# A graph kernel on one Trainium2 core: the first block issues three head weights and the indices only, the other loads follow in the main block, and ten node steps stand between gathering and messages

## The chip, the cores and the metric

One core of one Trainium2 chip. The metric is the device time of one launch in microseconds (us), lower is better. The engines: PE (TensorE, matrix products), DVE (VectorE), ACT (ScalarE), POOL (GpSimd) and SP (SyncE, which here only issues DMAs). Each has its own queue of instructions, in program order; they meet through semaphores.

## What is computed

Two layers of a graph network on 50,000 nodes with 256 features each and 12,500 edges, sorted by destination. The reference, cut:

```python
# layer 0: attention of 4 heads over the edges
h = einsum('ni,hid->nhd', x, W)
e = leaky(einsum('ehd,hd->eh', h[src], a_src) + einsum('ehd,hd->eh', h[dst], a_dst))
alpha = exp(minimum(e - segment_max(e)[dst], 20)); alpha /= segment_sum(alpha)[dst] + 1e-8
x = layernorm(x + segment_sum(alpha * h[src]).reshape(N, 256) @ W_out)
# layer 1: messages with edge attributes, a gate and a skip
m = x @ W_n2m.T; q, k, v = (m @ Wi.T + bi for i in 'qkv'); e = (edge_attr @ W_edge.T) @ We.T
out = segment_sum((v[src] + e) * segment_softmax(q[dst] . (k[src] + e) / sqrt(32)))
x_r = m @ Wskip.T + bskip
beta = sigmoid(concat(out, x_r, out - x_r) @ Wbeta.T)
x = layernorm(x + (beta * x_r + (1 - beta) * out) @ W_m2n.T)
```

Most nodes are the destination of no edge. For them both layers reduce to a layernorm, a product with 256 x 257 fixed weights, a sigmoid gate and a second layernorm.

## The kernel before

**Two kinds of work.** The *edge work* goes over 100 tiles of 125 edges, in stages: `Score` (gather rows of x by source and by destination with two indirect DMAs of POOL per tile, L824; transpose on PE, L847; project, L857 and L859; ACT copies to ST, L870, and to the store, L879; SP writes the gathered rows back, L835), a first `Softmax` (soft1), `Gather` (sum the weighted rows per destination, add to x, SP stores the rows, L1186), `Message` (gather again by source, L1308; normalize, L1473; keys, values, queries, L1368 to L1391), a second `Softmax` (soft2) and `Output`. The *node work* (`Nodes`) treats all 50,000 nodes as if they had no edge, in 196 steps of 256 rows: SP loads (L635), DVE measures (L763, L778), POOL takes the roots (L666, L671), ACT or DVE normalizes (L683 and L715, or L784), PE transposes (L734) and multiplies (L744), ACT and DVE gate and add (L696, L770), SP stores nine steps later (L651). Nodes with edges are overwritten by `Output` at the end. Step s loads the rows of step s + 2 into one of 12 slots; that load waits until the store that last used the slot has landed, and that store was issued in the step before.

**Set-up.** `head_pass` is the first block (L161 to L250). SP issues 24 loads: indices, the head weights `wh` and `attn`, all weights of layer 1, W_out, and, after a wait for DVE's memsets (L194), the borders of the tiles; ACT issues five loads of biases. PE turns the index rows and ACT copies them (L208, L209). A block ends for all engines when the last of them is done. All weights count on one semaphore, `c.ldd` (LOADS, L157). In the main block `Weights` (called `made`) derives the fused weights in five steps 0 to 4 between DVE and PE: DVE step 0 (L325 to L336, makes HEADS_READY), PE step 1 (transposes, L288 to L293), DVE step 1 (L338 to L353), PE step 2 (L300 to L302), DVE step 2 (L356 to L361), PE step 3 (L306, L307), DVE step 3 (L365), PE step 4 (L311 to L315), DVE step 4 (L370 to L388, makes NODES_READY, then ALL_READY). The first node product on PE waits for NODES_READY. `Masks` and `Positions` make the borders' masks and row positions on DVE; `Finder` looks up source rows. They use a scratch area in the store that the tiles from 72 on (FREE) overwrite.

**The order.** One plan, a list of (part, step), is made ahead by `order_of`, and every engine emits its instructions in this order. In the first stage `start_of` puts the steps of made, masks and positions at score steps written out by hand (MADE_AT, MASKS_AT, POSITIONS_AT, L1722 to L1724) and blends the first 74 node steps in from score step NODES_FROM on, the finder from FINDER_FROM on. For each later stage `blend` spreads a number of node steps (NODE_SHARE: 74 in the first stage, then 10, 66, 45, 10) evenly among the stage's own steps. The message stage has steps -6 to 102; at step -5 (A = 5) POOL waits until all rows of the gather stage are stored (L1302) and gathers the tiles' tails (L1305), and SP waits for these, writes them (L1335), waits for that write and then loads tile 0 (L1338). SP meets its node loads and stores in the same queue, in plan order.

```python
plan = start_of(entries[score], entries[finder], entries[nodes][0:at], entries[made], entries[masks], entries[positions])
for count, group in zip(share[1:], ((soft1,), (gather,), (message,), (soft2,))):
    lists = [entries[nodes][at:at + count]] + [entries[n] for n in group]
```

Of the kernel before, what the change touches and what calls it, by code (L numbers as in the profile page):

```python
# [153 lines left out]
        self.picked = take(TILES, P)  # L154


LOADS = 16 * (1 + 4 + 6 + 3 + 1 + 3 + 5)  # L157
EDGE_LOADS = 16 * 4


def head_pass(nc, c, ctx, io):  # L161
# [9 lines left out]
    with nc.Block() as block:  # L171
        @block.sync
        def _(sp):
            with nc.allow_non_contiguous_dma(reason="400 first and last dst of the tiles and a few short weight rows, once"):
                sp.dma_start(w.dsti, rows).then_inc(idx_loads, 16)
                sp.dma_start(w.srci, src.rearrange("(t e) -> t e", e=EDGES)).then_inc(idx_loads, 16)
                for k in range(2):
                    sp.dma_start(c.wh[:, k, 0:D].rearrange("p (h d) -> p h d", h=H),
                                 io["L0_gnn_W"][:, k * P:(k + 1) * P, :].rearrange("h i d -> i h d")).then_inc(c.ldd, 16)
                sp.dma_start(w.attn.rearrange("p h d -> p (h d)"),  # L180
                             io["L0_gnn_attn"].rearrange("(a h) d -> a (h d)", a=1).to_broadcast([P, H * 2 * HD])).then_inc(c.ldd, 16)
                for k, name in enumerate(("Wq", "Wk", "Wv", "Wskip")):
                    sp.dma_start(w.w_sq[:, k, :], io["L1_gnn_" + name]).then_inc(c.ldd, 16)
                for k in range(2):
                    sp.dma_start(w.w_m2n[:, k, :], io["L1_gnn_W_m2n"][k * P:(k + 1) * P, :]).then_inc(c.ldd, 16)
                sp.dma_start(w.w_e, io["L1_gnn_We"]).then_inc(c.ldd, 16)
                for k in range(3):
                    sp.dma_start(w.beta[:, k:k + 1], io["L1_gnn_Wbeta"][:, k * DM:(k + 1) * DM].rearrange("a d -> d a")).then_inc(c.ldd, 16)
                sp.dma_start(w.w_n2m, io["L1_gnn_W_n2m"]).then_inc(c.ldd, 16)
                for k in range(2):  # L190
                    sp.dma_start(w.w_edge[:, k, :], io["L1_gnn_W_edge"]).then_inc(c.ldd, 16)
                for k in range(2):
                    sp.dma_start(c.wo[:, k, :], io["L0_gnn_W_out"][k * P:(k + 1) * P, :]).then_inc(c.ldd, 16)
                sp.wait_ge(dve_done, 4)  # L194
                sp.dma_start(w.previ[1:TILES, :], rows[0:TILES - 1, EDGES - 1:EDGES]).then_inc(c.edge_loads, 16)
                sp.dma_start(w.nexti[0:TILES - 1, :], rows[1:TILES, 0:1]).then_inc(c.edge_loads, 16)
                for k, e in ((0, 0), (1, EDGES - 1)):
                    sp.dma_start(w.edgei[:, k, :], dst.rearrange("(a t e) -> a t e", a=1, e=EDGES)[:, :, e].to_broadcast([H, TILES])).then_inc(c.edge_loads, 16)

        @block.scalar  # L200
        def _(act):
            with nc.allow_non_contiguous_dma(reason="one bias column"):
                for out, name in ((w.bq_xr[:, 0:DM], "bq"), (w.bq_xr[:, DM:2 * DM], "bskip"), (w.b_kv[:, 0:DM], "bk"), (w.b_kv[:, DM:2 * DM], "bv")):
                    act.dma_start(out, io["L1_gnn_" + name].rearrange("(a d) -> a d", a=1).to_broadcast([P, DM])).then_inc(c.ldd, 16)
                act.dma_start(w.bs_cols[:, 0:1], io["L1_gnn_bskip"].rearrange("(d a) -> d a", a=1)).then_inc(c.ldd, 16)
            act.wait_ge(turned, 1)
            for k, out in enumerate((c.src_col, c.dst_col)):
                act.activation(out[:, :], c.psum[:, 0, k * 256:k * 256 + TILES], ACT.Copy).then_inc(turned, 1)  # L208
            act.activation(c.src_next[:, :], c.psum[:, 0, 0:TILES], ACT.Copy, bias=1.0).then_inc(turned, 1)  # L209
            act.wait_ge(turned, 4)  # L210

        @block.gpsimd
        def _(pool):
            own = Own(pool, pool_done)
            own(pool.memset(c.ident[:, :], 0.0))
            own.done()
            own(pool.affine_select(out=c.ident[:, :], in_=c.ident[:, :], compare_op=ALU.not_equal, fill=1.0,
                                   base=0, pattern=[[-1, P]], channel_multiplier=1))
            own(pool.memset(w.zero, 0.0))
            own(pool.memset(w.mean_w, 1.0 / D))  # L220
            own(pool.memset(c.half[:, :], -0.5))
            own(pool.memset(c.half5[:, :], -0.5))
            own(pool.memset(c.we2[:, :, :], 0.0))
            own(pool.iota(w.posi, [[1, EDGES]], base=1, channel_multiplier=P))
            own(pool.iota(w.basei, [[1, 1]], base=0, channel_multiplier=P))
            own(pool.iota(w.placei, [[1, EDGES]], base=1, channel_multiplier=0))
            own(pool.iota(c.own_pos[:, :], [[P, TILES]], base=0, channel_multiplier=1))
            own.done()

        @block.vector  # L230
# [12 lines left out]

        @block.tensor
        def _(pe):
            pe.wait_ge(pool_done, 2)
            pe.wait_ge(dve_done, 7)
            for k in range(2):
                last = pe.transpose(c.psum[:, 0, k * 256:k * 256 + TILES], w.row[:, k, :], c.ident[0:TILES, 0:TILES])
            last.then_inc(turned, 1)  # L250


class Weights:
# [2 lines left out]
    HEADS_READY, NODES_READY, ALL_READY = 1, 2, 3  # L256
    SPREAD, FUSED, MIXED = 20, 25, 28

    def __init__(self, nc, c, ctx):
        self.c = c  # L260

        def sem(name):
            return c.semaphore(nc, ctx, "weights_" + name)

        self.pe_done, self.own_sem, self.ready = (sem(n) for n in ("pe_done", "own_sem", "ready"))

    def sync(self, sp):
        def emit(s):
            return
        return emit  # L270

    def pool(self, pool):
# [10 lines left out]
    def tensor(self, pe):  # L283
        c, ps, w = self.c, self.c.psum, self.c.scratch

        def emit(s):
            if s == 1:
                pe.wait_ge(c.ldd, LOADS)  # L288
                for k in range(4):
                    pe.transpose(ps[:, 0, k * P:(k + 1) * P], w.w_sq[:, k, :], c.ident[:, :])  # L290
                for k in range(2):
# [27 lines left out]
    def vector(self, dve):  # L319
# [3 lines left out]

        def emit(s):
            if s == 0:  # L325
                dve.wait_ge(c.ldd, LOADS)
                for half, out in ((0, c.wh[:, :, D:HP]), (1, c.w_ad[:, :, :])):
                    own.done()
                    for k in range(2):
# [5 lines left out]
                own.done()  # L335
                dve.sem_inc(self.ready, 1)  # L336
            if s == 1:
                own(dve.tensor_tensor(w.wb, w.beta[:, 1:2], w.beta[:, 2:3], ALU.subtract))  # L338
                own(dve.tensor_tensor(w.wa, w.beta[:, 0:1], w.beta[:, 2:3], ALU.add))
                dve.wait_ge(self.pe_done, 1)  # L340
# [51 lines left out]
class Masks:  # L392
# [41 lines left out]

    def vector(self, dve):
        c, w = self.c, self.c.scratch
        own = Own(dve, self.own_sem)

        def emit(s):
            if s == 0:  # L440
# [45 lines left out]
class Positions:  # L486
# [3 lines left out]
    def __init__(self, nc, c, ctx, masks):  # L490
# [2 lines left out]
        def sem(name):  # L493
            return c.semaphore(nc, ctx, "positions_" + name)

        self.own_sem, self.asks, self.answers, self.ready, self.table = (sem(n) for n in ("own_sem", "asks", "answers", "ready", "table"))

    def sync(self, sp):
        def emit(s):
# [30 lines left out]

    def vector(self, dve):
        c, ps, w = self.c, self.c.psum, self.c.scratch
        own = Own(dve, self.own_sem)

        def emit(s):
            if s == 0:
# [711 lines left out]
class Message:  # L1248

    A = 5  # L1250
    B = 4
    FIRST, LAST = -6, TILES + 3

    def __init__(self, nc, c, ctx, io, made, positions, gather, finder):
        self.c, self.made, self.positions, self.gather, self.finder = c, made, positions, gather, finder
# [386 lines left out]
def main_pass(nc, c, io, out):  # L1642

    with ExitStack() as ctx:
# [4 lines left out]

        c.load_keeps = load_keeps  # L1650

        made = Weights(nc, c, ctx)
        masks = Masks(nc, c, ctx)
        positions = Positions(nc, c, ctx, masks)
        nodes = Nodes(nc, c, ctx, io["x"], out, made, NODE_NORMED, NODE_SCALED)
# [43 lines left out]
                    emits[n](s)  # L1699


NODE_SHARE = (74, 10, 66, 45, 10)
NODE_NORMED = ["A" if 74 <= s < 84 or s >= 186 else "AD"[s % 2] if s >= 84 else "D" for s in range(NSTEPS)]
NODE_SCALED = ["AD"[s % 2] if s < 66 else "A" for s in range(NSTEPS)]

# [1 line left out]
def order_of(parts, share):  # L1707
# [3 lines left out]
    entries = [[(n, s) for s in range(p.FIRST, p.LAST)] for n, p in enumerate(parts)]  # L1711
    at = share[0]
    plan = start_of(entries[score], entries[finder], entries[nodes][0:at], entries[made], entries[masks], entries[positions])
    for count, group in zip(share[1:], ((soft1,), (gather,), (message,), (soft2,))):
        lists = [entries[nodes][at:at + count]] + [entries[n] for n in group]
        at += count
        plan += [entry for _, entry in blend(lists)]
    assert at == len(entries[nodes])
    return plan + entries[output]


MADE_AT = (-5, -5, 0, 2, 4)  # L1722
MASKS_AT = (1, 6, 8, 10, 12)
POSITIONS_AT = (14, 16, 18, 20)  # L1724
NODES_FROM, FINDER_FROM = 2, 22


def start_of(score, finder, nodes, made, masks, positions):
# [22 lines left out]
def build(nc, io, out):  # L1751
    with ExitStack() as ctx:
        c = Core()
        c.ldd = c.semaphore(nc, ctx, "ldd")
        c.edge_loads = c.semaphore(nc, ctx, "edge_loads")

        def sb(name, shape, dt=F32):
# [85 lines left out]
```

## Time and profile before

| | us |
|---|---|
| median of 3 runs | 1377.34 (1364.89 to 1383.67) |
| the profiled execution | 1366.76, its span 1365.0 |
| PE busy in the span | 1197.2 |
| DVE, ACT, POOL busy | 1039.6, 810.9, 842.9 |

The profile shows one execution. Its span runs from the first to the last instruction; all times of the timeline count from its start. "Busy" leaves out waiting and issuing. Stages, roughly: start and scores to 400 us, soft1 to 450, gather to 733, messages to 1117, soft2 to 1150, output to the end. A row of the timeline merges several instructions of one line (xN).

### The profile page before, as it was taken

To read this page: it belongs to the slowest core of one execution; us is meant where nothing else is said; L and a number is where in the kernel's file an instruction comes from. 1 tells how busy PE (TensorE), PEld (TensorE's weight loads), DVE (VectorE), ACT (ScalarE), POOL (GpSimd) and SP (SyncE) were. 2 spreads that over 40 slices of the span, in tenths; PEclk is the share of its full clock that TensorE was granted. 3 is DMA by queue.
4 is the path that set the end of the run, shared out by engine and by line. 5 is a ranking of instruction groups with operands and counts; after the bars stand their busy time and mean duration, and the time that the engine had idled before them with its cause. 6 is when DMAs were issued, how large, how long until landed. Compare 5 with 4: busy or idle time off the path is not lost. (4 is left out here: it accounts for less than half of the span.)

```text
span 1365.0 us, 29010 instructions
## 1 busy us (share of the span) xinstructions
PE 1197.2 (88%) x7386; PEld 1061.5 (78%) x7386; DVE 1039.6 (76%) x3852; ACT 810.9 (59%) x2583; POOL 842.9 (62%) x1060
## 2 busy tenths in 40 slices
PE   3799999999995889899896999999999992988881
PEld 2688998989984777777775899999999982877771
DVE  3476777777779788898885888888888876877771
ACT  0366666666667756566565666666666675555652
POOL 4688888888843544455543666666666632377775
PEclk9899999999999999999999999999999996999996
DMA  6668888888853678787786766666666622555541
GB/s 161 193 186 262 285 253 274 264 272 264 268 185 116 185 228 238 236 246 240 240 243 202 222 209 198 192 201 197 199 197 185 200 93 98 158 176 169 172 155 58
DMA packets 208940, 277.09 MB, mean 203 GB/s; under 512 B 40060, under 2 KB 140563, under 8 KB 208777
## 3 DMA queue, kind: packets, MB, share of 16 engines
q1 hardware_dynamic: 188793, 224.13, 52.9%
q0 software_dynamic: 19264, 50.85, 13.1%
q8 instruction: 63, 1.03, 0.3%
q14 instruction: 100, 0.82, 0.2%
q10 hardware_dynamic: 720, 0.26, 0.1%
HBM read 159.73 MB, written 117.12 MB: 203 GB/s over the span
## 5 line engine op out<-in xcount | busy, mean ns | idle before, releaser
L744 PE MATMUL banks<-m_ext,node_XT 128*128 128x257 f32 x1568 | 377.9, 384 | 0.0
L744 PEld LDWEIGHTS banks<-m_ext,node_XT 128*128 128x128 f32 x1568 | 286.3, 193 | 32.9
L770 DVE SCALAR_TENSOR_TENSOR node_X<-banks,node_be,node_X 128x256 f32<-128x256 f32 x392 | 169.7, 474 | 79.2 <-ACT node_be L696 53.8
L671 POOL TENSOR_TENSOR node_r<-node_vv,half 128x4 f32<-128x4 f32 (+1 forms) x202 | 215.3, 1066 | 17.1 <-ACT node_X L683 0.3
L702 ACT ACTIVATE node_XT<-banks 128x512 f32<-128x512 f32 x196 | 117.2, 598 | 139.4 <-PE banks L734 125.2
L666 POOL TENSOR_SCALAR node_vv<-node_mv 128x4 f32<-128x4 f32 (+1 forms) x202 | 57.0, 282 | 212.4 <-DVE node_mv L778 196.9
L763 DVE BATCH_NORM_STATS2 node_st<-node_X 128x6 f32<-128x256 f32 x392 | 145.7, 413 | 20.7 <-DMA node_X<-in_x 19.3
L709 ACT ACTIVATE node_sq<-node_X 128x256 f32<-128x256 f32 x392 | 158.0, 409 | 0.0
L734 PE MATMUL banks<-ident,node_X 128*128 128x128 f32 x784 | 122.2, 279 | 28.5 <-DVE node_X L784 14.1
L683 ACT ACTIVATE node_X<-node_X,node_r 128x256 f32<-128x256 f32 x326 | 146.0, 496 | 1.4 <-POOL node_r L671 1.4
L824 POOL DMA_INDIRECT ring<-in_x,src_col x100 | 106.9, 1069 | 35.2 <-issue 14.2
L734 PEld LDWEIGHTS banks<-ident,node_X 128*128 128x128 f32 x784 | 95.8, 149 | 41.5 <-issue 19.5
L1531 POOL DMA_INDIRECT out<-ring,last_col x100 | 102.5, 1025 | 35.3 <-issue 21.9
L1308 POOL DMA_INDIRECT ring<-rows,src_pos x100 | 105.7, 1057 | 22.3 <-issue 20.4
L824 POOL DMA_INDIRECT ring<-in_x,dst_col x100 | 97.3, 973 | 31.4 <-issue 31.4
L857 PE MATMUL banks<-wh,ST 128*128 128x260 f32 x400 | 107.5, 392 | 9.1 <-ACT store L879 8.0
L870 ACT ACTIVATE ST<-banks 128x512 f32<-128x512 f32 x100 | 59.7, 597 | 86.9 <-PE banks L847 38.6
L1383 PE MATMUL banks<-w_kv,ST 128*128 128x256 f32 x400 | 103.1, 380 | 0.2 <-DVE store L1436 0.2
L1217 PE MATMUL banks<-wo,AT 128*128 128x256 f32 x400 | 102.9, 380 | 0.0
L1243 DVE TENSOR_TENSOR_SCAN AT<-MB,AT,banks 128x128 f32<-128x128 f32 x198 | 83.9, 465 | 19.1 <-PE banks L1210 15.2
L784 DVE TENSOR_SCALAR node_X<-node_X,node_mv,node_r 128x256 f32<-128x256 f32 x250 | 90.5, 403 | 0.0
L1568 PE MATMUL banks<-w_out,S 128*128 128x256 f32 x200 | 63.4, 399 | 24.3 <-DVE AT L1621 19.4
(262 smaller groups left out, 2773.4 us busy)
## 6 DMA issues: line engine op xcount, KB each, us to landing
node_X<-in_x SPq DMA_DIRECT2D x196, 256.0 KB
out<-node_X SPq DMA_DIRECT2D x196, 256.0 KB
ring<-rows SPq DMA_DIRECT2D x300, 128.0 KB
rows<-ring SPq DMA_DIRECT2D x100, 256.0 KB
rows<-ring SPq DMA_DIRECT2D x200, 128.0 KB
MB<-keeps SPq DMA_DIRECT2D x40, 320.0 KB, 5.5
MB<-picks SPq DMA_DIRECT2D x50, 128.0 KB
MB<-in_src SPq DMA_DIRECT2D x25, 195.3 KB
```

Source lines behind the costliest of these rows:

```text
L671: pool.tensor_tensor(r[:, s % 4, NT * lo:NT * hi], v, self.c.half[:, NT * lo:NT * hi], ALU.pow).then_inc(self.roots, 1)
L683: last = eng.activation(row, row, ACT.Identity, scale=rz)
L702: act.activation(self.XT[:, n % 2, :], c.psum[:, 4, 0:NT * D], ACT.Copy, bias=1.0).then_inc(self.xt_ready, 1)
L709: last = act.activation(self.sq[:, k, :], X[:, n % U, k, :], ACT.Square, scale=1.0 / D ** 0.5, accum_out=self.mv[:, s % 4, 1, k, 1:2])
L734: last = pe.transpose(ps[:, 4, k * D + h * P:k * D + (h + 1) * P], self.X[:, n % U, k, h * P:(h + 1) * P], c.ident[:, :])
L744: last = pe.matmul(ps[:, NT * o + k, 0:D + 1], self.XT[:, o, k * D + h * P:k * D + (h + 1) * P], c.m_ext[:, h, :], start=(h == 0), stop=(h ...
L763: last = dve.bn_stats(st[:, s % 2, k, :], X[:, s % U, k, :])
L770: last = dve.scalar_tensor_tensor(out=X[:, n % U, k, :], in0=ps[:, b + k, 0:D], scalar=self.be[:, n % 4, k:k + 1], in1=X[:, n % U, k, :], ...
L824: pool.indirect_dma_start(out=c.ring[:, n % R, side, :], out_offset=None, in_=self.x, in_offset=bass.IndirectOffsetOnAxis(ap=col[:, n:n + ...
L857: pe.matmul(ps[:, 6, 0:HP], c.ST[:, o, h * P:(h + 1) * P], c.wh[:, h, :], start=(h == 0), stop=(h == 1))
L1308: pool.indirect_dma_start(out=c.ring[:, n % R, 1, :], out_offset=None, in_=c.rows, in_offset=bass.IndirectOffsetOnAxis(ap=c.src_pos[:, n:n ...
L1383: pe.matmul(ps[:, 6, 0:2 * DM], c.ST[:, o, h * P:(h + 1) * P], c.w_kv[:, h, :], start=(h == 0), stop=(h == 1))
```

## The change

The first block keeps, on SP, the indices, `wh` and `attn` (counted on a new semaphore, `head_loads`), and ACT issues what PE's step 1 of the weights reads (`turn_loads`; the two parts of W_m2n in one DMA). The other 16 loads (12 on `ldd`, four of borders on `edge_loads`) are issued by SP in the main block, as step 0 of made, which stands ahead of score step -5. PE's step 1 waits for `turn_loads`, DVE's step 0 for `head_loads`, DVE's step 1 for `ldd`. The hand-written places move. The node steps of the message stage, 45, are split: 4 alone behind the gather stage, 6 blended with message steps -6 to -1, 35 with the rest. Masks and positions share one counting semaphore.

```diff
-LOADS = 16 * (1 + 4 + 6 + 3 + 1 + 3 + 5)
+HEAD_LOADS = 16 * 3
+TURN_LOADS = 16 * 7
+LOADS = 16 * 12
@@ head_pass, SP
                 for k in range(2):
                     sp.dma_start(c.wh[:, k, 0:D]...,
-                                 ...).then_inc(c.ldd, 16)
+                                 ...).then_inc(c.head_loads, 16)
                 sp.dma_start(w.attn..., ...
-                             ...).then_inc(c.ldd, 16)
-                ...
-                sp.wait_ge(dve_done, 4)
-                ...
+                             ...).then_inc(c.head_loads, 16)
@@ head_pass, ACT
-                for out, name in ((w.bq_xr[:, 0:DM], "bq"), (w.bq_xr[:, DM:2 * DM], "bskip"), (w.b_kv[:, 0:DM], "bk"), (w.b_kv[:, DM:2 * DM], "bv")):
-                    act.dma_start(out, ...).then_inc(c.ldd, 16)
-                act.dma_start(w.bs_cols[:, 0:1], ...).then_inc(c.ldd, 16)
+            for k, name in enumerate(("Wq", "Wk", "Wv", "Wskip")):
+                act.dma_start(w.w_sq[:, k, :], io["L1_gnn_" + name]).then_inc(c.turn_loads, 16)
+            act.dma_start(w.w_m2n, io["L1_gnn_W_m2n"].rearrange("(k p) d -> p k d", p=P)).then_inc(c.turn_loads, 16)
+            act.dma_start(w.w_e, io["L1_gnn_We"]).then_inc(c.turn_loads, 16)
+            act.dma_start(w.w_n2m, io["L1_gnn_W_n2m"]).then_inc(c.turn_loads, 16)
@@ Weights.sync
+            if s == 0:
+                    for k in range(3):
+                        sp.dma_start(w.beta[:, k:k + 1], ...).then_inc(c.ldd, 16)
+                    sp.dma_start(w.bs_cols[:, 0:1], ...).then_inc(c.ldd, 16)
+                    for k in range(2):
+                        sp.dma_start(w.w_edge[:, k, :], ...).then_inc(c.ldd, 16)
+                    sp.dma_start(w.previ[1:TILES, :], ...).then_inc(c.edge_loads, 16)
+                    sp.dma_start(w.nexti[0:TILES - 1, :], ...).then_inc(c.edge_loads, 16)
+                    for k, e in ((0, 0), (1, EDGES - 1)):
+                        sp.dma_start(w.edgei[:, k, :], ...).then_inc(c.edge_loads, 16)
+                    for out, name in (... "bq", "bskip", "bk", "bv" ...):
+                        sp.dma_start(out, ...).then_inc(c.ldd, 16)
+                    for k in range(2):
+                        sp.dma_start(c.wo[:, k, :], ...).then_inc(c.ldd, 16)
@@ Weights.tensor, s == 1
-                pe.wait_ge(c.ldd, LOADS)
+                pe.wait_ge(c.turn_loads, TURN_LOADS)
@@ Weights.vector
             if s == 0:
-                dve.wait_ge(c.ldd, LOADS)
+                dve.wait_ge(c.head_loads, HEAD_LOADS)
             if s == 1:
+                dve.wait_ge(c.ldd, LOADS)
@@ Positions
-        own = Own(dve, self.own_sem)
+        own = self.masks.own
@@ Message
-    FIRST, LAST = -6, TILES + 3
+    FIRST, EARLY, LAST = -6, 0, TILES + 3
@@ order_of
-NODE_SHARE = (74, 10, 66, 45, 10)
+NODE_SHARE = (74, 10, 66, 4, 6, 35, 10)
-    for count, group in zip(share[1:], ((soft1,), (gather,), (message,), (soft2,))):
-        lists = [entries[nodes][at:at + count]] + [entries[n] for n in group]
+    first = Message.EARLY - Message.FIRST
+    stages = ((entries[soft1],), (entries[gather],), (), (entries[message][:first],), (entries[message][first:],), (entries[soft2],))
+    for count, group in zip(share[1:], stages):
+        lists = [entries[nodes][at:at + count]] + [e for e in group]
@@ the places in the first stage
-MADE_AT = (-5, -5, 0, 2, 4)
-MASKS_AT = (1, 6, 8, 10, 12)
-POSITIONS_AT = (14, 16, 18, 20)
-NODES_FROM, FINDER_FROM = 2, 22
+MADE_AT = (-5, -3, 0, 1, 3)
+MASKS_AT = (4, 7, 9, 11, 14)
+POSITIONS_AT = (13, 15, 17, 20)
+NODES_FROM, FINDER_FROM = 3, 20
```

## Rows read from the trace of the kernel before

**Rows 1.** The page, first part: busy time, share of the span, instructions.

```profile
PE 1197.2 (88%) x7386; PEld 1061.5 (78%) x7386; DVE 1039.6 (76%) x3852; ACT 810.9 (59%) x2583; POOL 842.9 (62%) x1060
```

**Rows 2.** Windows: stretch, its length, busy us (count) of PE, PEld, DVE, ACT, POOL, clock, DMA, GB/s.

```profile
30.00:40.00 10.00, 3.32 (x19) 2.48 (x17) 1.48 (x7) 0.60 (x1) 6.65 (x7) 0.91 0.95 312
...
740.00:750.00 10.00, 0.46 (x3) 0.20 (x2) 2.42 (x10) 0.98 (x4) 4.42 (x6) 0.74 0.69 195
...
900.00:1000.00 100.00, 100.00 (x706) 93.82 (x705) 87.44 (x366) 63.13 (x192) 63.74 (x80) 1.00 0.67 198
```

**Rows 3.** Timeline from 0 us: start, duration, engine, line, tiles, [idle before <-releaser].

```profile
3.11 1.28 ACT L208 ACT_TABLE_LOAD   x1 [3.11 <-issue]
...
5.55 1.29 SPq L183 DMA_DIRECT2D store<-in_L_gnn_Wskip  x1
...
13.70 0.97 SPq L198 DMA_DIRECT2D store<-in_dst  x2
...
15.20 0.76 DVE L330 TENSOR_TENSOR store<-wh,store 128x256 f32<-128x256 f32 x2 [10.39 <-PEq L171]
...
15.98 1.16 POOL L824 DMA_INDIRECT ring<-in_x,src_col  x1 [13.26 <-POOLq L171]
```

**Rows 4.** DMA issues by tile: engine, count, size, median us to landing.

```profile
wo<-in_L_gnn_W_out SPq DMA_DIRECT2D x2, 128.0 KB, 2.2
```

**Rows 5.** Timeline, 18 to 60 us: weights, gathers, stores, first node step.

```profile
18.46 0.16 DVE L338 TENSOR_TENSOR store<-store 128x1 f32<-128x1 f32 x1
...
31.14 1.11 PE L306 MATMUL banks<-w_out,store 128*128 128x257 f32 x4
...
37.53 0.95 POOL L824 DMA_INDIRECT ring<-in_x,dst_col  x1 [0.30 <-issue]
...
41.39 0.39 ACT L879 ACTIVATE store<-banks 128x260 f32<-128x260 f32 x1 [7.85 <-remote]
...
42.82 6.59 SPq L835 DMA_DIRECT2D rows<-ring  x2
...
57.32 0.63 PE L734 MATMUL banks<-ident,node_X 128*128 128x128 f32 x4 [0.61 <-DVE node_X L784]
```

**Rows 6.** Timeline of SP's queue, 732 to 746 us.

```profile
732.80 0.33 SPq L635 DMA_DIRECT2D node_X<-in_x  x1
...
736.31 0.33 SPq L635 DMA_DIRECT2D node_X<-in_x  x1
736.74 0.38 SPq L651 DMA_DIRECT2D out<-node_X  x1
...
739.92 0.35 SPq L635 DMA_DIRECT2D node_X<-in_x  x1
...
741.97 0.30 SPq L1335 DMA_DIRECT2D rows<-AT  x1
745.30 0.32 SPq L1338 DMA_DIRECT2D ring<-rows  x1
```

**Rows 7.** Timeline of POOL, 733 to 738 us.

```profile
737.71 1.15 POOL L1305 DMA_INDIRECT AT<-rows,tail_pos  x1 [2.36 <-issue]
```

**Rows 8.** Timeline of DVE and PE, 735 to 763 us.

```profile
735.69 0.75 DVE L763 BATCH_NORM_STATS2 node_st<-node_X 128x6 f32<-128x256 f32 x2 [0.67 <-DMA node_X<-in_x]
...
747.54 0.75 DVE L1446 BATCH_NORM_STATS2 message_st<-ring 128x6 f32<-128x256 f32 x2 [10.17 <-DMA ring<-rows]
...
755.12 0.38 PE L1368 MATMUL banks<-ident,ring 128*128 128x128 f32 x2
...
760.13 0.60 PE L734 MATMUL banks<-ident,node_X 128*128 128x128 f32 x4
...
762.31 0.38 PE L1368 MATMUL banks<-ident,ring 128*128 128x128 f32 x2
```

**Rows 9.** Timeline of PE, 417 to 422 us (the softmax stage).

```profile
417.76 0.63 PE L734 MATMUL banks<-ident,node_X 128*128 128x128 f32 x4 [0.58 <-issue]
...
420.89 0.63 PE L734 MATMUL banks<-ident,node_X 128*128 128x128 f32 x4 [0.76 <-issue]
```

More of the change, by code:

```diff
@@ L173, in _ @@
         def _(sp):
-            with nc.allow_non_contiguous_dma(reason="400 first and last dst of the tiles and a few short weight rows, once"):
+            with nc.allow_non_contiguous_dma(reason="short rows of the head weights"):
                 sp.dma_start(w.dsti, rows).then_inc(idx_loads, 16)
@@ L178, in _ @@
                     sp.dma_start(c.wh[:, k, 0:D].rearrange("p (h d) -> p h d", h=H),
-                                 io["L0_gnn_W"][:, k * P:(k + 1) * P, :].rearrange("h i d -> i h d")).then_inc(c.ldd, 16)
+                                 io["L0_gnn_W"][:, k * P:(k + 1) * P, :].rearrange("h i d -> i h d")).then_inc(c.head_loads, 16)
                 sp.dma_start(w.attn.rearrange("p h d -> p (h d)"),
-                             io["L0_gnn_attn"].rearrange("(a h) d -> a (h d)", a=1).to_broadcast([P, H * 2 * HD])).then_inc(c.ldd, 16)
@@ L182, in _ @@
[L182 to L193, printed above, removed]
-                sp.wait_ge(dve_done, 4)
-                sp.dma_start(w.previ[1:TILES, :], rows[0:TILES - 1, EDGES - 1:EDGES]).then_inc(c.edge_loads, 16)
@@ L196, in _ @@
-                sp.dma_start(w.nexti[0:TILES - 1, :], rows[1:TILES, 0:1]).then_inc(c.edge_loads, 16)
-                for k, e in ((0, 0), (1, EDGES - 1)):
-                    sp.dma_start(w.edgei[:, k, :], dst.rearrange("(a t e) -> a t e", a=1, e=EDGES)[:, :, e].to_broadcast([H, TILES])).then_inc(c.edge_loads, 16)
+                             io["L0_gnn_attn"].rearrange("(a h) d -> a (h d)", a=1).to_broadcast([P, H * 2 * HD])).then_inc(c.head_loads, 16)
         @block.scalar
         def _(act):
-            with nc.allow_non_contiguous_dma(reason="one bias column"):
-                for out, name in ((w.bq_xr[:, 0:DM], "bq"), (w.bq_xr[:, DM:2 * DM], "bskip"), (w.b_kv[:, 0:DM], "bk"), (w.b_kv[:, DM:2 * DM], "bv")):
-                    act.dma_start(out, io["L1_gnn_" + name].rearrange("(a d) -> a d", a=1).to_broadcast([P, DM])).then_inc(c.ldd, 16)
-                act.dma_start(w.bs_cols[:, 0:1], io["L1_gnn_bskip"].rearrange("(d a) -> d a", a=1)).then_inc(c.ldd, 16)
+            for k, name in enumerate(("Wq", "Wk", "Wv", "Wskip")):
+                act.dma_start(w.w_sq[:, k, :], io["L1_gnn_" + name]).then_inc(c.turn_loads, 16)
@@ L257, with __init__ @@
     SPREAD, FUSED, MIXED = 20, 25, 28
-    def __init__(self, nc, c, ctx):
-        self.c = c
+    def __init__(self, nc, c, ctx, io):
+        self.nc, self.c, self.io = nc, c, io
         def sem(name):
@@ L267, in sync @@
     def sync(self, sp):
+        nc, c, w, io = self.nc, self.c, self.c.scratch, self.io
+        dst = io["dst"]
+        rows = dst.rearrange("(t e) -> t e", e=EDGES)
         def emit(s):
-            return
+            if s == 0:
+                with nc.allow_non_contiguous_dma(reason="400 first and last dst of the tiles and a few short weight rows, once"):
+                    for k in range(3):
+                        sp.dma_start(w.beta[:, k:k + 1], io["L1_gnn_Wbeta"][:, k * DM:(k + 1) * DM].rearrange("a d -> d a")).then_inc(c.ldd, 16)
+                    sp.dma_start(w.bs_cols[:, 0:1], io["L1_gnn_bskip"].rearrange("(d a) -> d a", a=1)).then_inc(c.ldd, 16)
+                    for k in range(2):
+                        sp.dma_start(w.w_edge[:, k, :], io["L1_gnn_W_edge"]).then_inc(c.ldd, 16)
+                    sp.dma_start(w.previ[1:TILES, :], rows[0:TILES - 1, EDGES - 1:EDGES]).then_inc(c.edge_loads, 16)
+                    sp.dma_start(w.nexti[0:TILES - 1, :], rows[1:TILES, 0:1]).then_inc(c.edge_loads, 16)
+                    for k, e in ((0, 0), (1, EDGES - 1)):
+                        sp.dma_start(w.edgei[:, k, :], dst.rearrange("(a t e) -> a t e", a=1, e=EDGES)[:, :, e].to_broadcast([H, TILES])).then_inc(c.edge_loads, 16)
+                    for out, name in ((w.bq_xr[:, 0:DM], "bq"), (w.bq_xr[:, DM:2 * DM], "bskip"), (w.b_kv[:, 0:DM], "bk"), (w.b_kv[:, DM:2 * DM], "bv")):
+                        sp.dma_start(out, io["L1_gnn_" + name].rearrange("(a d) -> a d", a=1).to_broadcast([P, DM])).then_inc(c.ldd, 16)
+                    for k in range(2):
+                        sp.dma_start(c.wo[:, k, :], io["L0_gnn_W_out"][k * P:(k + 1) * P, :]).then_inc(c.ldd, 16)
         return emit
@@ L436, in vector @@
         c, w = self.c, self.c.scratch
-        own = Own(dve, self.own_sem)
+        own = self.own = Own(dve, self.own_sem)
         def emit(s):
@@ L494, in sem @@
             return c.semaphore(nc, ctx, "positions_" + name)
-        self.own_sem, self.asks, self.answers, self.ready, self.table = (sem(n) for n in ("own_sem", "asks", "answers", "ready", "table"))
+        self.asks, self.answers, self.ready, self.table = (sem(n) for n in ("asks", "answers", "ready", "table"))
     def sync(self, sp):
@@ L532, in vector @@
         c, ps, w = self.c, self.c.psum, self.c.scratch
-        own = Own(dve, self.own_sem)
+        own = self.masks.own
         def emit(s):
@@ L1650, in main_pass @@
         c.load_keeps = load_keeps
-        made = Weights(nc, c, ctx)
+        made = Weights(nc, c, ctx, io)
         masks = Masks(nc, c, ctx)
@@ L1753, in build @@
         c = Core()
-        c.ldd = c.semaphore(nc, ctx, "ldd")
+        c.ldd, c.head_loads, c.turn_loads = (c.semaphore(nc, ctx, n) for n in ("ldd", "head_loads", "turn_loads"))
         c.edge_loads = c.semaphore(nc, ctx, "edge_loads")
```

## The prediction

> **What bounds the kernel now.** Read first the busy shares, then the windows, then the two places in time that the diff touches. TensorE (PE) is busy 1197.2 of 1365.0 us, 88% [rows 1]; in the message stage a window of 100 us shows it at 100.00 us [rows 2]. So in the long stages PE is the bound, and PE work can't be made shorter by moving it, only moved into holes. The windows show two holes that the diff touches. One is the start: PE works 3.32 us between 30 and 40 us, while the DMA engines are 0.95 busy [rows 2]. The other is the change from gathering to messages: PE works 0.46 us between 740 and 750 [rows 2].
>
> Of the start the timeline gives the parts. The first block ends when SP has issued its last load (13.70 + 0.97 = 14.67), and DVE starts the next block at 15.20, POOL its first gather at 15.98 [rows 3]. Then a chain runs through the weights: DVE L338 at 18.46, PE L306 at 31.14 [rows 5]. ACT's L879 waits for PE's L859, which the trace puts before L306; yet ACT is released only at 41.39, with 7.85 us of idle time that the profile puts down to no instruction ("remote") [rows 5]. I read this as PE's results coming out late, or not being seen; the trace doesn't say why. It ends 2.9 us after POOL's last gather of the first burst (37.53 + 0.95 = 38.48) [rows 5]. Steady work begins with the first node step, at 57.32 [rows 5].
>
> Of the second hole: after the gather stage SP stands in a chain of DMAs. The tails are gathered (POOL, 737.71) [rows 7], SP stores them 4.26 us later (741.97), waits for the store and loads tile 0 at 745.30 [rows 6], DVE has it at 747.54 after 10.17 us of idle time, and PE's first message is at 755.12 [rows 8].
>
> **The start, step by step.** SP's block now ends after five issues instead of 24. ACT issues seven loads, where it had five. One issue takes from 0.49 (0.97 for two, L198) to 1.29 us (L183 at 5.55) [rows 3], so seven end between 4.1 and 9.7 us. Behind them stand the table load, 1.28 us [rows 3], and three short activations; with about 2.3 us for these the block ends between 6.4 and 12. I take 6.8, near the short issue, since ACT's queue has fewer packets ahead of it than SP's had. With the same 0.53 us from block end to DVE (14.67 to 15.20) and 0.78 more to POOL [rows 3], gathers begin at 8.1, 7.9 us earlier (bounds 2.7 and 8.3).
>
> What doesn't come earlier is the chain of weights. Its second step (DVE L338) now waits for the twelve loads on ldd, and these stand among 16 issues at the head of SP's queue in the main block: 7.3 + 16 x 0.49 = 15.1, and the last (wo) needs 2.2 us to land [rows 4], 17.3 in all. Before, the step began at 18.46 [rows 5]. The 16 issues now run beside the gathers, and where the DMA engines are full SP took 6.59 us for two issues (L835 at 42.82) [rows 5]. I take 18.5 for the step, no change; bounds 17.3 and, at 1.1 us an issue, 27. All that SP has behind these issues (stores of gathered tiles, node loads) is due only when gathers have landed, near 15 us, so the 16 cost it nothing if they end there. The head weights (HEADS_READY) come earlier, but PE's first product stands behind the second weight step, so nobody uses that.
>
> The gain is the burst. POOL runs 18 gathers from 15.98 to 38.48, 1.25 us each; with NODES_FROM at 3 it runs 20 before its first node step, from 8.1 to 33.1. If the late results end 2.9 us after it, as they do now, ACT goes on at 36.0 instead of 41.39: 5.4 us earlier. Behind that the last weight step stands one score step earlier, and one more tile stands ahead of the first node step; I set these equal. So the first node step comes at 51.9 instead of 57.32, and PE is full from there: minus 5.4. Bounds: if the results aren't late at all, 8.7 us go (32.7, the end of L306 and L307, to 41.4) and somewhat more with the earlier last step, minus 11; if the late loads take 27, plus 6 (8.5 later, less an estimated 2.5, since the burst is over by then and its late results no longer add).
>
> **The change of stages, step by step.** Before, three node steps stand ahead of message step 0 and 42 behind it; now ten and 35. In the full message stage a node step costs PE 2.18 us (L734 at 760.13 to the next tile's L1368 at 762.31) [rows 8]; seven fewer save 15.3 us there. That is the gain side, and it is firm, since PE is at 100% (bounds 14 and 16.5).
>
> Against it: ten node steps with nothing else run at their own pace p. SP sets it: the load of a step waits for the store of the step before to land, and 736.74 to 739.92 is 3.18 us; step to step it is 3.5 to 3.6 (732.80, 736.31, 739.92) [rows 6]. In the softmax stage, without the gather stage's rows, steps follow at 3.13 us (417.76 to 420.89) [rows 9]. I take p = 3.3, bounds 2.9 and 3.9.
>
> Follow SP. Its last step of the gather stage is at 736.31; step 155, behind which the tails now stand, ends at 737.1 + 6p = 756.9 (six steps on). POOL gathers the tails after its part of step 155, near 752, and they land by then too. Then, as before, 3.33 us for the store of the tails (741.97 to 745.30), 0.8 us to the next node load, one p for the load after it, 2.89 us until DVE has that (732.80 to 735.69) [rows 6, 8], and about 4 us for DVE's rest of node and message steps up to PE's step 0 (half of the 7.58 from 747.54 to 755.12). Sum: 737.1 + 3.3 + 0.8 + 2.9 + 4.1 + 7p = 748.2 + 7p = 771.3. Before it was 755.12: 16.2 us later, against 15.3 saved: plus 0.9. With p = 2.9 it is minus 1.8, with 3.9 plus 5. So ten steps fill the hole, but node steps alone run at 3.3 us where PE would do them in 2.18 between messages, and that eats what the hole gives.
>
> The Trainium skill has a rule here: by "DMA: Bandwidth & Descriptors", section "Anatomy of one DMA", a DMA takes about 2.0 us plus its bytes at 436 GB/s (fitted there on DMAs that POOL issues), which for 256 KB would be 2.6 us instead of the row's 3.18, p near 3.0 and the stage minus 1; the trace is slower than the rule in this place.
>
> **At nothing.** The masks, positions and finder move by a few score steps; all stand beside a PE that is full, and are first needed at tile 72, hundreds of us later (price if that failed: a few us, once). The shared count of positions and masks, two semaphores more and one less, and the joined m2n load cost nothing that I can see; bounds plus and minus 0.5.
>
> **Sum.** Minus 5.4 plus 0.9 is minus 4.5: of the profiled execution's 1366.8 us, 1362.3. That execution is 10.6 us below the median of the runs shown; on the median, 1377.3, it is 1372.8.
>
> **Rivals.** (a) PE's late results go away with the new order of work, since made step 3 no longer stands behind tile 1: minus 11 and plus 0.9, 1367. For it: the later parts of the trace show no such wait. Against: the same burst of gathers and stores runs over the same chain, only earlier. (b) The second hole fills well: with the lighter traffic stores land sooner, p is near 2.8, PE's step 0 at 767.8: minus 2.6 there and minus 5.4 at the start, 1369. For it: 3.13 in the softmax stage; against: messages' loads go through the same queue. (c) The late loads are slowed by the gathers. It decides from the landing of wo: beyond 18.5 us each us is lost, beyond about 24 (the issues at 0.95 us each) the start is slower than before. At 1.1 us each the start is plus 6, with plus 0.9 the time is 1384, slower than before. For it: the 0.95 DMA share and SP's 6.59 us; against: 16 loads are few bytes. (d) The start does nothing: the late results end at 41.4 whatever comes before: 1378.
>
> **How the numbers follow.** Forecast 0.42, (a) 0.15, (b) 0.15, (c) 0.13, (d) 0.15. All lie within 1% of each other, and the runs shown of the kernel before spread over 1364.9 to 1383.7. The range is 1359 to 1385: (a) at its low end with some spread, (c) at its high end. About 2% (27.5 us) is what a measurement of this kernel can tell from no change; none of the cases reaches it. Faster by more than that, 0.05, if (a) and (b) hold together and more; slower, 0.04; within, 0.91.
>
> **What would show it.** Right: POOL's first gather near 8 us; DVE L338 near 18.5 though DVE's first step starts near 10; the long wait of ACT L879 ending near 36; the first node step near 52; SP's node loads about 3.3 us apart through the second hole, PE's first message step about 35 us after the gather stage's last node load, and the message stage some 15 us shorter from its step 0. Wrong: a first node step beyond 57, or before 49; node steps apart by more than 3.9 or less than 2.9; PE idle for 5 us in one piece in the second hole; a message stage in which PE has idle time, so that seven fewer node steps save less than 14.

## The result and the profile after

The changed kernel takes 1378.66 us in the median of 12 runs (1372.98 to 1382.6), against 1373.88 for the kernel before, measured beside it in 12 runs (1364.89 to 1383.82). The ratio is 1.0071, with an interval of 1.0053 to 1.009: slower by 0.7%, within the 2% that I had given 0.91, and inside the range of 1359 to 1385, but on the other side of no change than the forecast (1372.8 of 1377.3, a ratio of 0.997). The runs of the kernel before lie in two groups, and 1.0071 is the changed kernel's mean, 1378.3, over that of the seven runs up to 1377.34, 1368.6, while the medians of all runs give 1.0035. So the size of the loss isn't firm from these runs alone; that there is one rests also on the experiments below.

The profiled execution took 1382.16 us, with a span of 1380.3; that of before was 1366.76, near the low end of its runs. The two traces differ by 15 us, the medians by 4.8, so the traces serve for the order of things and the durations of steps, not for the sum.

The page of the changed kernel, busy time; PE has 12.7 us more than in [rows 1], for the same instructions:

```profile
PE 1209.9 (88%) x7386; PEld 1066.7 (77%) x7386; DVE 1044.2 (76%) x3852; ACT 809.5 (59%) x2583; POOL 842.5 (61%) x1060
```

Its windows, in the columns of [rows 2]:

```profile
30.00:40.00 10.00, 2.16 (x7) 1.64 (x6) 2.10 (x5) 0.60 (x1) 1.89 (x2) 0.61 0.93 339
...
740.00:750.00 10.00, 6.55 (x35) 5.10 (x34) 5.72 (x24) 7.00 (x24) 3.96 (x6) 1.00 0.52 159
...
900.00:1000.00 100.00, 99.90 (x706) 93.43 (x705) 86.39 (x363) 61.06 (x183) 63.74 (x78) 1.00 0.66 194
```

The first hole is emptier than before (PE 2.16 of 10 us instead of 3.32). The second is filled, though not full: 6.55 instead of 0.46. The message stage is as full as it was, with the same 706 matmuls in 100 us.

**The start.** Timeline of the changed kernel, 0 to 60 us, against [rows 3, 5]:

```profile
6.38 1.29 SPq L262 DMA_DIRECT2D store<-in_L_gnn_Wbeta  x3
...
7.20 1.31 POOL L829 DMA_INDIRECT ring<-in_x,src_col  x1 [4.47 <-POOLq L173]
...
14.38 0.91 SPq L273 DMA_DIRECT2D wo<-in_L_gnn_W_out  x2
15.34 6.35 SPq L840 DMA_DIRECT2D rows<-ring  x3
...
21.62 0.16 DVE L343 TENSOR_TENSOR store<-store 128x1 f32<-128x1 f32 x1 [11.45 <-DMA wo<-in_L_gnn_W_out]
...
31.45 0.95 POOL L829 DMA_INDIRECT ring<-in_x,dst_col  x1 [0.30 <-issue]
...
35.80 0.42 DVE L362 COPY store<-banks 128x256 f32<-128x256 f32 x1 [11.14 <-remote]
35.86 0.60 ACT L875 ACTIVATE ST<-banks 128x512 f32<-128x512 f32 x1 [29.90 <-remote]
...
37.99 2.08 PE L310 MATMUL banks<-w_out,store 128*128 128x257 f32 x4 [7.84 <-DVE we L366]
...
58.37 0.63 PE L739 MATMUL banks<-ident,node_X 128*128 128x128 f32 x4 [0.49 <-DVE node_X L789]
```

POOL gathers 8.8 us earlier than before (7.20 for 15.98), and SP has issued the last late load at 15.29. But DVE's second weight step, L343 here, waits 11.45 us for `wo` and starts at 21.62, where L338 started at 18.46: 3.2 us later. The late results are there again ("remote"), and end at 35.86. PE's step 3 of the weights, L310, which stood ahead of them at 31.14, now stands behind them at 37.99: it waits for DVE's L366, and DVE saw PE's step 2 only at 35.80 (L362). The first node step comes 1.05 us later than before, not 5.4 earlier.

**The change of stages.** SP's queue in the changed kernel, 736 to 769 us, against [rows 6]:

```profile
736.05 0.33 SPq L640 DMA_DIRECT2D node_X<-in_x  x1
...
743.17 0.33 SPq L640 DMA_DIRECT2D node_X<-in_x  x1
743.61 0.38 SPq L656 DMA_DIRECT2D out<-node_X  x1
746.77 0.33 SPq L640 DMA_DIRECT2D node_X<-in_x  x1
747.20 0.38 SPq L656 DMA_DIRECT2D out<-node_X  x1
750.77 0.33 SPq L640 DMA_DIRECT2D node_X<-in_x  x1
...
758.87 0.35 SPq L640 DMA_DIRECT2D node_X<-in_x  x1
...
759.79 0.31 SPq L1340 DMA_DIRECT2D rows<-AT  x1
762.50 0.32 SPq L1343 DMA_DIRECT2D ring<-rows  x1
...
763.35 0.42 SPq L640 DMA_DIRECT2D node_X<-in_x  x1
...
768.13 0.33 SPq L640 DMA_DIRECT2D node_X<-in_x  x1
```

POOL's gather of the tails, DVE's first look at a message tile and PE's first message there, against [rows 7, 8]:

```profile
752.99 1.15 POOL L1310 DMA_INDIRECT AT<-rows,tail_pos  x1 [0.22 <-issue]
...
764.56 0.75 DVE L1451 BATCH_NORM_STATS2 message_st<-ring 128x6 f32<-128x256 f32 x2 [0.71 <-DMA ring<-rows]
...
775.18 0.44 PE L1373 MATMUL banks<-ident,ring 128*128 128x128 f32 x2 [2.23 <-DVE ring L1478]
```

From 736.05, the last load of the gather stage, to 758.87, the last one ahead of the tails, there are six node steps, 3.8 us each (3.6 to 4.0, and the last 4.5); the next takes 4.8 (763.35 to 768.13). A store stands right behind each load, and each load waits for the store that was issued behind the load before it. The waits of SP's queue from 728 to 785 us, as a sum, a count and the longest:

```profile
SPq L640 <- DMA out<-node_X: 33.9, 13, 3.6
```

PE's message step 0 starts at 775.18 instead of 755.12, 20.1 us later. From there to the end of the last message tile's transposes it is 347.6 us instead of 358.7: 11.1 us are saved.

### The profile page after: what moved, and what is told of

The parts are those of the page before. It is cut to its first block and busy times, and to the rows that moved or that the text cites. A ratio compares the mean times of both kernels' runs of the same rounds, so it can differ in the third digit from the quotient of the medians.

```text
span 1380.3 us, 29009 instructions
## 1 busy us (share of the span) xinstructions
PE 1209.9 (88%) x7386; PEld 1066.7 (77%) x7386; DVE 1044.2 (76%) x3852; ACT 809.5 (59%) x2583; POOL 842.5 (61%) x1060
## 5 line engine op out<-in xcount | busy, mean ns | idle before, releaser
L1573 PE MATMUL banks<-w_out,S 128*128 128x256 f32 x200 | 64.8, 407 | 27.1 <-DVE AT L1626 20.2
```

## The experiments

They ran in three comparisons (`start_only`, `stages_only`, `start_gated` and `before_again`, then the two other edits of the start and the two with `AHEAD = 1`, then the last four), each on a chip of its own. The kernel before took 1343.66, 1341.09 and 1342.1 us there, against 1373.88 above; so I take them for other chips than the one of the two kernels above, which isn't on record. Ratios are against its runs in the same comparison, and marks in time are compared among these runs alone.

**The start and the regrouping, each alone.** `start_only` is the changed kernel with the stages of before:

```diff
-NODE_SHARE = (74, 10, 66, 4, 6, 35, 10)
+NODE_SHARE = (74, 10, 66, 45, 10)
-    stages = (..., (entries[gather],), (), (entries[message][:first],), (entries[message][first:],), ...)
+    stages = (..., (entries[gather],), (entries[message],), ...)
```

> The change with its stage split undone (45 node steps in the message stage again): only the new start. Theory A (the loss is the change of stages): 0 to +4 us against before, ratio 0.998 to 1.003; first message transpose on PE about 26 us after the gather stage's last sum, as before. Theory B (the loss is the start, the late loads): +7 to +11 us, ratio near 1.007.

It took 1348.1 us: 1.0039 [1.0022, 1.0056]. `stages_only` is the kernel before with the same edit the other way round (and `EARLY = 0`).

> The kernel before with only the node steps regrouped (4, 6, 35). Theory A: +7 to +10 us, ratio near 1.006; PE's first message transpose about 45 us after the gather stage's last sum instead of 26, and the message stage from there shorter by 11 to 12 us. Theory B: 0 to +2 us.

It took 1349.25 us: 1.005 [1.0033, 1.0067]. Both halves cost time. Their sum, 0.89%, lies in the interval of the whole change, 0.53% to 0.9%; it is more than the 0.35% of the medians, so this is a rough check only. For reference, `before_again` is the kernel before, unchanged, traced beside them.

> The kernel before, unchanged, for a second trace: its runs fall into two groups, near 1367 and near 1382 us. If this one is of the slow group, the stage in which it loses shows where the 15 us come from; expected: the output stage (195 us in the first trace, 201 in that of the changed kernel), and a start within 2 us of the first trace.

It took 1344.41 us, one run, and the 15 runs of the kernel before beside it lie between 1339.07 and 1346.6; so where the 15 us that I asked for come from stays open. Its start isn't within 2 us of the first trace either, and the trace has no late results at all. PE in `before_again`, the first node step:

```profile
44.29 0.63 PE L734 MATMUL banks<-ident,node_X 128*128 128x128 f32 x4 [0.61 <-DVE node_X L784]
```

That is 13 us earlier than in [rows 5], though its DVE L338 starts at 18.6 as there. So my 5.4 us rested on a disturbance that isn't there in every execution. In `start_only` the chain is undisturbed too, and yet the first node step comes at 52.18, 7.9 us later than in `before_again`: the second weight step starts 3.8 us later (22.44 for 18.62), and from there to the first node step it takes 4.1 us longer. Its DVE, POOL and PE:

```profile
22.44 0.19 DVE L343 TENSOR_TENSOR store<-store 128x1 f32<-128x1 f32 x1 [12.11 <-DMA wo<-in_L_gnn_W_out]
...
47.52 0.34 POOL L671 TENSOR_SCALAR node_vv<-node_mv 128x2 f32<-128x2 f32 x1 [15.34 <-DVE node_mv L783]
...
52.18 0.63 PE L739 MATMUL banks<-ident,node_X 128*128 128x128 f32 x4 [0.46 <-DVE node_X L789]
```

PE's first message, in `before_again` and in `stages_only`:

```profile
746.66 0.43 PE L1368 MATMUL banks<-ident,ring 128*128 128x128 f32 x2
```

```profile
766.76 0.69 PE L1368 MATMUL banks<-ident,ring 128*128 128x128 f32 x2 [3.72 <-DVE ring L1473]
```

The last rows of the gather stage are done at 719.0 in `stages_only` and at 719.1 in `before_again`. From there to message step 0 it is 47.8 us against 27.5: 20.2 longer. From step 0 to the end of the last message transposes it is 344.0 us against 357.9: 14.0 saved. The net of 6.3 fits the 6.7 us of the ratio.

**Are the gathers what delays the loads and the results?** `start_gated` is `start_only` with POOL held after two tiles until PE has done step 3 of the weights.

```diff
+                if n == 2:
+                    pool.wait_ge(self.made.pe_done, 3)
```

> start_only, but POOL holds the gathers of tiles 2 and up until PE's third weight step is done. Theory A1 (PE's results come out late because the burst of gathers, stores and node loads fills the DMA engines): no idle time of ACT or DVE put down to nothing above 1 us in the first 60 us, wo landed by 18 us instead of 21.6, PE's fourth weight step near 36 us instead of 45; in all 3 to 8 us faster than start_only if the gathers held back don't run late. Rival A2 (late results come with PE's cold clock or the profile, not with the burst): the same 5 us of late results near 30 us, and the time no better than start_only.

It took 1353.36 us: 1.0073 [1.0055, 1.0092]. DVE's second weight step came at 19.65 instead of 22.44, so with four gathers beside the loads instead of a full burst `wo` lands 2.8 us sooner, at the same time of issue; but the tiles then come late, the first node step at 54.58. On the late results it says nothing, since `start_only` has none either, and the 3 to 8 us that I expected didn't come.

**What of the start costs?** Two edits of `start_only`. `start_old_places` puts the hand-written places back to those of before:

```diff
-MADE_AT = (-5, -3, 0, 1, 3)
-MASKS_AT = (4, 7, 9, 11, 14)
-POSITIONS_AT = (13, 15, 17, 20)
-NODES_FROM, FINDER_FROM = 3, 20
+MADE_AT = (-5, -5, 0, 2, 4)
+MASKS_AT = (1, 6, 8, 10, 12)
+POSITIONS_AT = (14, 16, 18, 20)
+NODES_FROM, FINDER_FROM = 2, 22
```

> start_only with the hand-written places of before (weights, masks, positions, node and finder start). Theory P (half of the start's loss is the places: one more tile and the masks ahead of the first node steps while POOL's gathers stop at the same wait): first node transpose on PE about 4 us earlier than in start_only (48 instead of 52.2), 2 to 4 us faster than start_only. Theory L (all of it is the late landing of the loads): within 1 us of start_only, DVE's second weight step at 22.4 in both.

It took 1342.22 us: 1.0007 [0.9993, 1.0021], no difference from before. Issue to landing in it, and then its POOL and PE:

```profile
wo<-in_L_gnn_W_out SPq DMA_DIRECT2D x2, 128.0 KB, 6.7
```

```profile
36.41 0.24 POOL L671 TENSOR_SCALAR node_vv<-node_mv 128x2 f32<-128x2 f32 x1 [6.70 <-DVE node_mv L783]
...
46.95 0.63 PE L739 MATMUL banks<-ident,node_X 128*128 128x128 f32 x4 [0.62 <-DVE node_X L789]
```

`wo` took 6.7 us to land, where [rows 4] has 2.2. The second weight step is as late as in `start_only` (22.1), but from there to the first node step it is 24.8 us instead of 29.7. With the new places the last step of the weights stands ahead of the first node step in DVE's queue; POOL stands 15.34 us at that node step's root instead of 6.70, and gathers nothing from 32.19 to 49.00. The run moved all the places at once; that this one makes the difference is read from the traces, not tested alone. `start_split_loads` gives the loads that DVE's step 1 doesn't read (four biases and W_out) a semaphore of their own, waited for at its step 4:

```diff
-LOADS = 16 * 12
+LOADS = 16 * 6
+REST_LOADS = 16 * 6
+            if s == 4:
+                dve.wait_ge(c.rest_loads, REST_LOADS)
```

> start_only, but the biases and W_out count on a semaphore of their own that only DVE's last weight step waits for; its second step waits for the six loads issued first. Theory L: that step comes near 12 to 14 us instead of 22.4, PE's second step near 16 instead of 25.6, and the start ends 8 to 12 us earlier than in start_only, 4 to 8 us ahead of before (ratio 0.994 to 0.997). Theory D (the DMA engines are full from 15 us on and the gathers and node loads set the start): the weight steps come early but the first node transpose stays above 46 and the time within 3 us of start_only.

It took 1338.22 us: 0.9966 [0.9946, 0.9986], faster than before and 0.7% faster than `start_only`. Waits of DVE up to 62 us in `start_only` and in `start_split_loads`:

```profile
DVE store L343 <- DMA wo<-in_L_gnn_W_out: 12.1, 1, 12.1
```

```profile
DVE store L344 <- DMA store<-in_L_gnn_W_edge: 0.6, 1, 0.6
```

One wait of 12.1 us becomes 0.6; the step starts at 10.80, and the first node step follows at 41.03:

```profile
10.80 0.16 DVE L344 TENSOR_TENSOR store<-store 128x1 f32<-128x1 f32 x1 [0.60 <-DMA store<-in_L_gnn_W_edge]
```

```profile
41.03 0.63 PE L741 MATMUL banks<-ident,node_X 128*128 128x128 f32 x4 [0.56 <-DVE node_X L791]
```

**Is it the store ahead of each load that sets the pace?** `AHEAD = 1` makes step s load the rows of step s + 1, so the slot's last store was issued one step earlier than with 2 and has a step more to land. `before_ahead1` is the kernel before with it, `stages_ahead1` is `stages_only` with it.

```diff
-    AHEAD = 2
+    AHEAD = 1
```

> The kernel before with node loads one step ahead, as the reference for stages_ahead1. Theory S: both softmax stages and the tail of gathering a little faster, 2 to 6 us less than before; then stages_ahead1 loses less against this one (0 to +3 us) than stages_only against before (+6.7). Theory E: within 2 us of before.

> stages_only with node loads issued one step ahead instead of two, so that a load's slot was stored two steps before and SP doesn't wait for that store to land. Theory S (the pace of node steps that stand alone, 3.6 us, is SP's: load after the landing of the last store): pace 2.7 to 3.1 us between gathering and messages, PE's first message transpose 4 to 6 us earlier than in stages_only (767), 4 us or more faster than stages_only. Theory E (the engines' own chain DVE, POOL, ACT, PE sets the pace): pace 3.4 to 3.6 as before, same time or a little slower, DVE waiting for loads.

They took 1332.53 us, 0.9927 [0.9902, 0.9951], and 1332.5 us, 0.9932 [0.9911, 0.9953]; on the kernel before that is more than the 2 to 6 us expected. The waits of SP's queue from 400 to 1100 us, in `before_again`, `stages_only`, `before_ahead1` and `stages_ahead1`:

```profile
SPq L635 <- DMA out<-node_X: 124.7, 70, 5.1
```

```profile
SPq L635 <- DMA out<-node_X: 150.2, 78, 5.0
```

```profile
SPq L635 <- DMA out<-node_X: 2.7, 2, 2.0
```

```profile
SPq L635 <- DMA out<-node_X: 3.9, 3, 1.5
```

The wait for the stores' landing is all but gone in both. More than half of it comes back as a wait of SP's stores for the rows that ACT finishes (L683), in `before_again` and in `before_ahead1`:

```profile
SPq L53 <- ACT node_X L683: 51.2, 28, 5.5
```

```profile
SPq L53 <- ACT node_X L683: 120.4, 66, 7.6
```

SP's loads in `stages_ahead1`, between gathering and messages:

```profile
711.05 0.43 SPq L635 DMA_DIRECT2D node_X<-in_x  x1
...
713.21 0.43 SPq L635 DMA_DIRECT2D node_X<-in_x  x1
...
716.71 0.43 SPq L635 DMA_DIRECT2D node_X<-in_x  x1
...
718.86 0.43 SPq L635 DMA_DIRECT2D node_X<-in_x  x1
...
722.37 1.42 SPq L635 DMA_DIRECT2D node_X<-in_x  x1
```

Four steps take 11.3 us (711.05 to 722.37), 2.8 each; all six (707.90 to 726.23) take 3.1 each, where `stages_only` has 3.9 (727.10 to 750.26). The regrouping is then neither a loss nor a gain in the times: the way to message step 0 grows by 18.6 us (22.5 to 41.1), and the message stage shrinks by 16.6 (358.3 to 341.7). And the store-to-load wait was worth 0.7% on the kernel before, most of it ahead of the message stage (the gather stage ends at 708.3, and at 719.1 in `before_again`).

**Together.** `best_of_both` is the kernel before with the new start, the loads split, the old places and `AHEAD = 1`. `best_with_split` adds the regrouping (4, 6, 35), `best_new_places` the new places instead, `best_split_short` a shorter regrouping:

```diff
-NODE_SHARE = (74, 10, 66, 45, 10)
+NODE_SHARE = (74, 10, 66, 0, 6, 39, 10)
```

> The kernel before with the new start, its loads split (start_split_loads), the old places, and node loads one step ahead; stages as before. If the three effects add (split loads about -10 us against start_only, old places -4, one step ahead -9 against before): ratio about 0.984 to 0.989, first node transpose on PE near 37. If the places don't matter once the weights are early: about 0.989 to 0.991.

> best_of_both with the node steps regrouped (4, 6, 35). With node steps at a pace of about 2.8 us instead of 3.6 the regrouping should cost nothing and bring nothing: within 2 us of best_of_both. If the regrouping is bad in itself: 4 us or more slower.

> best_of_both with the new hand-written places. If the places cost by themselves (a tile more and the masks ahead of the first node steps): 2 to 4 us slower than best_of_both, first node transpose near 41. If they cost only when the weights are late: within 1 us.

> best_of_both with no node step alone, six blended with message steps -6 to -1, 39 behind. The tails are then asked for after two node steps instead of six, and three steps more than before stand in the hole. By the sum of the prediction with a pace of 2.8 us: three to four node steps fewer in the message stage save 7 to 9 us, the way to PE's first message grows by 4 to 8; 0 to 4 us faster than best_of_both. If every node step in the hole costs what it saves: within 1 us.

| | us | against before |
|---|---|---|
| `best_of_both` | 1323.76 | 0.987 [0.9853, 0.9888] |
| `best_with_split` | 1325.68 | 0.9873 [0.9852, 0.9894] |
| `best_new_places` | 1324.28 | 0.9869 [0.9852, 0.9885] |
| `best_split_short` | 1320.84 | 0.9857 [0.9833, 0.988] |

All four beat the kernel before by over 1%, and with four runs each they can't be told from each other. So within about 3 us the new places cost nothing once the weights come early, though the first node step still comes 3.4 us later (39.95 for 36.60 in `best_of_both`), and the regrouping of ten or of six node steps neither costs nor gains. The ratio of `best_of_both` is the one expected if the places count too, but `best_new_places` reaches the same without the old ones.

## Why the prediction was wrong

**The block and the first gather**: right, and a little better than my 8.1: gathers begin at 7.20, 8.8 us earlier, where my bound was 8.3. SP's sixteen issues end at 15.29, where I had 15.1; they began 0.9 us sooner than I took and needed 0.56 us each, not 0.49.

**"I take 18.5 for the step, no change"**: failed, 21.6 here and 22.4 in `start_only`. What I took over wrongly was the 2.2 us of landing from [rows 4], a row from a time when no gathers ran. Beside the gathers it is 6.7 (`start_old_places`), and 4.8 with the gathers held back (`start_gated`), so part of the rise isn't theirs by any run here. This is rival (c)'s mechanism, but in the landing of the data, not in the issues, and at less than half its size (3.2 us for 8.5). Its cause in the code is the shared count: step 1 reads neither W_out nor the biases that it waited for, as `start_split_loads` shows. I had named the wait and not asked which of the twelve loads the step needs.

**"If the late results end 2.9 us after it"**: they end at 35.86, where I had 36.0, partly by luck (the last gather ends at 32.40 instead of 33.1, and the results come 3.5 us behind it). It was worth nothing: PE's third step of the weights came to stand behind them, and the traces of the experiments, which show no late results, show a loss all the same. I had taken a disturbance of one execution as a part of the kernel; for rival (a) I even wrote that the later parts of the trace show no such wait, but ACT has seven more of them between 60 and 400 us, 12.6 us in all. What makes PE's results late isn't settled. They stand in the two traces of the first chip and in none of the twelve of the experiments, so no run has them and lacks the gathers.

**"I set these equal"** (last weight step earlier against one more tile): failed. With late weights the new places cost 4.9 us from the second weight step to the first node step (29.7 against 24.8), and 0.3% of the whole (1.0039 against 1.0007, each in its own comparison). With early weights they cost nothing (`best_new_places`).

So the start, forecast at minus 5.4, is plus 5.2 (0.39% of 1343.7). With the loads split it is a gain (`start_split_loads`, 0.9966).

**Saved in the message stage, 15.3 us**: 14.0 in the undisturbed pair, at my lower bound; between the first two traces it was 11.1, beyond it, and no run shows where the 3 us between the two are.

**"I take p = 3.3"**: the term of the stage's sum that was mis-sized. The six node steps took 3.8 us each, and the seventh p, for the load behind the tails, took 4.8; over all seven that is 3.94. My own rows had 3.5 to 3.6 [rows 6], and I had leaned on the softmax stage's 3.13, where no edge rows were stored; even 3.6 would have given only 773.4. With 3.94 my sum, 748.2 + 7p, gives 775.8, less 0.6 for a store of the tails that took 2.7 us instead of 3.3; measured was 775.2. Message step 0 came 20.1 us later, not 16.2. The Trainium skill's rule, in "DMA: Bandwidth & Descriptors", section "Anatomy of one DMA" (2.0 us plus the bytes at 436 GB/s, an estimate of 2.6 us for 256 KB), would have made p near 3.0 and the stage a gain of 1 us. The trace is slower than that: from the issue of a store to the next load it is 3.1 to 4.1 us (3.16 from 743.61 to 746.77). The measurement decides. So the stage's plus 0.9 was plus 6.7 in `stages_only`, in which my case for 3.9 (plus 5) comes nearest. That the pace is set by the store's landing is shown by `AHEAD = 1`.

**The signs.** Three of the signs of being wrong that I had named are there: the first node step is beyond 57 (58.37), node steps lie more than 3.9 us apart (4.0 and 4.5), and the message stage saves less than 14 us between the first two traces (11.1). Idle time of 5 us in one piece on PE in the second hole isn't; the longest there is 2.4.

**The rivals.** (a) and (b) didn't come. (c), 1384 or a ratio of 1.005, is nearest to the ratio, and its plus 6 for the start is near the plus 5.2; but that is in part luck, since its mechanism came at less than half its size and the places made up the rest. (d), 1378, hits the time, but its ratio is 1.0007 and its reason doesn't hold: the start does something, and it is a loss. **Masks, positions, semaphores at nothing**: nothing in the runs speaks against it beyond the places above.

## What to carry to other kernels

A semaphore shared by loads makes its first reader wait for the last of them: when loads are moved beside bulk gathers, split the count by who reads first, and price the landing from a row with that traffic. Work moved into a hole runs at the pace of its own slowest loop, so look for that loop (here a load that waits for a store issued one step earlier), measure its pace over all the steps that will stand there, and lengthen it before moving the work. A wait that the profile can't name, seen in one execution, is to be looked for in a second one before it carries a forecast.

## What was not expected of the hardware

The same kernel took 1373.9 us in the first comparison and 1341 to 1344 in the others, and PE's late results stood in the traces of the first alone: products that the changed kernel's trace ends at 29.56 and 30.15 were seen by DVE at 35.80 and by ACT at 35.86 ("remote"). Whether that is the chip or a state of it, and whether these waits make the 30 us, no run shows. The granted clock between 740 and 750 us was 0.74 [rows 2] in the kernel before, where PE worked 0.46 us there, and 1.00, the level of 2.4 GHz, in the changed one, where it worked 6.55; no gain from it shows, since SP's loads set the pace of that stretch.
